# Second cross attention's keys and values from high and low parts, with the gates' weights in a place that is already used

## The reference, cut to what matters

```python
x = x + L0_xattn(layernorm(x), ctx, ctx, mask)
x = x + L0_attn(layernorm(x))       # convolutions, delta rule by chunks of 32, gates by W_fuse1, mixing
x = x + L0_ffn(layernorm(x))        # 8 experts, the two best of each row
x = x + L1_xattn(layernorm(x), ctx, ctx)
x = x + L1_attn(layernorm(x))
x = x + L1_ffn(layernorm(x))        # 16 experts of 128 and a shared one
# L1_xattn: 16 heads of 16
k = ctx @ Wk.T + bk                 # keys and values of all 64 contexts:
v = ctx @ Wv.T + bv                 # this is what the change forms in another way
out = softmax(q @ k.T / 4) @ v @ Wo.T + bo
```

## Time and profile before

| what | us |
|---|---|
| median of 3 runs (lowest, highest) | 1621.93 (1618.51, 1623.67) |
| span of the profiled execution | 1609.7 |
| TensorE busy | 1490.3 (93%) |
| VectorE busy | 1100.2 (68%) |
| ScalarE busy | 813.9 (51%) |
| GpSimd busy | 583.5 (36%) |
| keys' and values' matmuls (L386 and L390), busy | 121.5 + 117.2 |

### The profile page before, as it was taken

How to read it: one execution, slowest core, us unless ns; L and a number is a source line. 1 busy time by engine, 2 the same in 40 slices (tenths; PEclk the granted TensorE clock), 3 DMA queues, 4 the chain that set the end, 5 groups by cost and what they waited for, 6 DMA issues and landing times. The chain is left out here.

```text
span 1609.7 us, 38473 instructions
## 1 busy us (share of the span) xinstructions
PE 1490.3 (93%) x15176; PEld 1144.1 (71%) x15176; DVE 1100.2 (68%) x2412; ACT 813.9 (51%) x1848; POOL 583.5 (36%) x487
## 2 busy tenths in 40 slices
PE   5998999989988999999999989999899788999998
PEld 3454468544456579999998646666688686799997
DVE  4588869974047456666563558888599676767887
ACT  1233742121143336666654449999277422766663
POOL 2440310000011026777645346787288452121210
PEclk9899999999999999999999989999999999999999
DMA  9993048532024357676658317664000010010001
GB/s 327 316 354 97 1 156 219 133 73 46 1 80 137 110 209 278 217 274 239 237 181 222 96 50 246 204 209 129 27 1 1 18 30 15 1 34 21 27 1 53
DMA packets 114074, 203.99 MB, mean 127 GB/s; under 512 B 38073, under 2 KB 74361, under 8 KB 108009
## 3 DMA queue, kind: packets, MB, share of 16 engines
q1 hardware_dynamic: 91481, 107.72, 22.5%
q0 software_dynamic: 10032, 57.55, 10.3%
q10 hardware_dynamic: 12384, 36.27, 6.8%
HBM read 161.67 MB, written 39.83 MB: 125 GB/s over the span
## 5 line engine op out<-in xcount | busy, mean ns | idle before, releaser
L2387 POOL TENSOR_TENSOR a_pr<-a_pr,a_inv 128x1028 f32<-128x1028 f32 x64 | 122.2, 1909 | 63.6 <-DVE a_inv L2515 63.6
L386 PE MATMUL ps<-kv_ctx,kv_w 128*128 128x257 f32 x464 | 121.5, 397 | 8.5 <-ACT kv_kv L410 3.0
L390 PE MATMUL ps<-kv_w,kv_ctx 128*128 128x256 f32 x464 | 117.2, 397 | 8.3 <-ACT kv_kv L410 8.3
L2479 ACT ACTIVATE a_pr<-ps,a_neg 128x257 f32<-128x257 f32 x256 | 119.0, 473 | 2.7 <-DVE a_neg L2531 2.3
L2531 DVE TENSOR_REDUCE a_neg<-ps 128x2 f32<-128x514 f32 x128 | 87.9, 688 | 41.9 <-PE ps L2404 40.9
L1631 POOL TENSOR_TENSOR b0m_pm<-b_dr,b_gates 128x256 f32<-128x256 f32 x16 | 13.2, 829 | 279.3 <-SPq L1595 250.4
L390 PEld LDWEIGHTS ps<-kv_w,kv_ctx 128*128 128x128 f32 x464 | 89.4, 199 | 28.8 <-ACT kv_kv L410 14.6
L386 PEld LDWEIGHTS ps<-kv_ctx,kv_w 128*128 128x128 f32 x464 | 86.7, 197 | 26.8 <-issue 13.6
L3389 DVE SCALAR_TENSOR_TENSOR x<-ps,g_gate,x 128x256 f32<-128x256 f32 x256 | 105.1, 475 | 0.0
L972 DVE SCALAR_TENSOR_TENSOR b_F<-b_F,b_fir 128x992 f32<-128x992 f32 (+29 forms) x128 | 96.7, 792 | 0.0
L2415 PE MATMUL ps<-ident,a_pr 128*128 128x128 f32 x512 | 81.2, 281 | 16.3 <-ACT a_prT L2486 10.9
(11 more groups left out here) (447 smaller groups left out, 4433.1 us busy)
## 6 DMA issues: line engine op xcount, KB each, us to landing
late_kv<-kv SPq DMA_DIRECT2D x52, 513.0 KB, 4.4
kv<-kv_kv ACTq DMA_DIRECT2D x46, 513.0 KB, 5.4
a_ctxT<-in_ctxT SPq DMA_DIRECT2D x32, 514.0 KB, 9.7
a_ctxR<-in_ctx SPq DMA_DIRECT2D x32, 512.0 KB
kv_ctx<-in_ctxT ACTq DMA_DIRECT2D x34, 257.0 KB, 3.4
kv_ctx<-in_ctxT SPq DMA_DIRECT2D x24, 257.0 KB, 4.6
outs<-f_yo SPq DMA_DIRECT2D x16, 256.0 KB, 4.5
a_vB<-vlast SPq DMA_DIRECT2D x32, 128.0 KB
```

The source lines that it names most:

```text
L386: done = e.matmul(out[:, 0:NK], self.w[:, 0, c, cols(part)], ctx[:, c, :], start=(c == 0), stop=(c == DC - 1))
L390: done = e.matmul(out[:, cols(t, D)], ctx[:, c, cols(t)], self.w[:, 1, c, :], start=(c == 0), stop=(c == DC - 1))
L2387: e.tensor_tensor(pr[:, b % RP, :, :], pr[:, b % RP, :, :], inv[:, b % 2, :].unsqueeze(2).to_broadcast([P, HG, NK]), ALU.mult).then_inc(*p ...
L2479: e.activation(pr[:, b % RP, r, :], K.ps[:, bank(b, r), 0:NK], ACT.Exp, bias=neg[:, b % 2, r:r + 1], accum_out=tot[:, b % 2, r:r + 1]).the ...
```

## The change

The context and the two weights of the second cross attention's keys and values are split into high and low parts, and `product3` forms each product of a batch: 24 products of type float32r in place of 8 in float32, the keys' with 258 columns (`WIDTH`), the last of them zero.

- The raw weights are loaded ahead of the contexts of tile 14 in the first attention; GpSimd copies them to the high part and subtracts.
- For every context ScalarE rounds it into a high part (`round_to`), and GpSimd, or VectorE in the experts' tail (`low_by_dve`), subtracts for the low part (`low`). There are two places of parts (`LEAD = 2`), three in the router. ScalarE rounds a batch after the eviction of the batch two before it.
- TensorE waits for the low part in place of the load. The context's next load waits for it too, and ScalarE issues it behind the batch's store.
- The places of parts take 8 KB a partition. For them `W_fuse1` no longer has a tile of its own in `delta_solve`: it goes into `qk[:, 2:4]`, which the gram tiles read, and SP issues its load behind all stores of pairs and loads of A and M and behind the last gram tile. The squares and one row of the projections also go into tiles in use.
- In `delta_solve` GpSimd makes 20 low parts, in `delta_mix` one for each pair of tiles. In `experts_0` low parts stand between its gathers. In the experts' tail VectorE makes one low part behind each gather sum, and the two places of parts lie in the experts' weights.

SP's queue in `delta_solve`, before. (In what follows, `x4` counts like rows; a name behind "waits" is the semaphore waited for, named by who used it first, as `dma_a0_4_keys1` for the landing of the pairs' stores.)

The diff, cut to its core:

```diff
-    SLOTS, MORE = 3, 3
+    SLOTS, MORE, LEAD = 3, 3, 2
     BY_SYNC, TAIL, QUERIES = sum(AHEAD[:3]) + SLOTS, sum(AHEAD[:4]), sum(AHEAD[:5])
+    WIDTH = NK + 1
     def __init__(self, Y):
         self.K, self.Y = Y.K, Y
-        self.w, self.bk = Y.sb("w", [P, 2, DC, D]), Y.sb("bk", [P, DC])
+        self.w = [Y.sb(f"w{n}", [P, 2, DC, D], F32R) for n in "HL"]
+        self.bk = Y.sb("bk", [P, DC])
         self.ctx = places(Y.sb("ctx", [P, self.SLOTS, DC, NK]))
...
                         for b in range(B)]
-        self.loaded = self.BY_SYNC
+        self.loaded = 0
         self.mm, self.ev = Y.sig("pe", "kv"), Y.sig("act", "kv")
+        self.high, self.w_split = Y.sig("act", "kvhigh"), Y.sig("pool", "kvw")
+        self.p_low, self.v_low = Y.sig("pool", "kvlow"), Y.sig("dve", "kvlow")
         self.own = [KvPlace(Y, at, f"kv{n}") for n, at in enumerate(places(Y.sb("kv", [P, 2, KV])))]
-        self.formed = self.taken = self.last = 0
-        self.hosts = []
+        self.formed = self.taken = self.last = self.rounded = self.lowered = 0
+        self.hosts, self.parts = [], []
+        self.low_by_dve = range(self.TAIL, self.QUERIES)
     def host(self, count, banks, kv):
...
         return [h for h in self.hosts if h[0] <= j][-1]
+    def split_into(self, first, places):
+        self.parts.append((first, places))
+    def split_of(self, b):
+        first, at = [x for x in self.parts if x[0] <= b][-1]
+        return at[(b - first) % len(at)]
+    def split_before(self, b):
+        first, at = [x for x in self.parts if x[0] <= b][-1]
+        return b - len(at) if b - len(at) >= first else None
+    def low_done(self, b):
+        early, n = min(b, self.TAIL - 1) + 1, self.QUERIES - self.TAIL
+        if b in self.low_by_dve:
+            return self.v_low.at(b - self.TAIL + 1)
+        return self.p_low.at(early if b < self.TAIL else b + 1 - n)
     def before(self, b):
...
         s = self.slot_of[b]
+        if self.before(b):
+            e.wait_ge(*self.low_done(self.before(b)[-1]))
         e.dma_start(self.ctx[s], self.K.ins["ctxT"][b // BT, :, b % BT, :, :]).then_inc(*self.ld_c[s].up(16))
+        self.loaded = b + 1
     def sync(self, e, n):
         for b in range(self.loaded, min(self.loaded + n, B)):
-            if self.before(b):
-                e.wait_ge(*self.mm.at(3 * self.before(b)[-1] + 3))
             self.load(e, b)
-            self.loaded = b + 1
-    def begin(self, e):
+    def load_weights(self, e, raw):
         for n, name in enumerate(("Wk", "Wv")):
-            e.dma_start(self.w[:, n, :, :], features(self.K.ins[f"L1_xattn_{name}T"])).then_inc(*self.ld_w.up(16))
+            e.dma_start(raw[:, n, :, :], features(self.K.ins[f"L1_xattn_{name}T"])).then_inc(*self.ld_w.up(16))
         e.dma_start(self.bk[:, :], self.K.ins["L1_xattn_bk"]).then_inc(*self.ld_w.up(16))
-        for b in range(self.SLOTS):
-            self.load(e, b)
+    def split_weights(self, e, raw):
+        e.wait_ge(*self.ld_w.at(48))
+        e.tensor_copy(self.w[0][:, :, :, :], raw[:, :, :, :]).then_inc(*self.w_split.up())
+        e.wait_ge(*self.w_split.at(1))
+        e.tensor_tensor(self.w[1][:, :, :, :], raw[:, :, :, :], self.w[0][:, :, :, :].bitcast(F32), ALU.subtract).then_inc(*self.w_split.up())
+    def clear(self, e, first):
+        for at in [x for x in self.parts if x[0] == first][0][1]:
+            for part in at:
+                e.memset(part[:, :, NK:self.WIDTH].bitcast(F32), 0.0)
+    def round_to(self, e, last):
+        for b in range(self.rounded, last):
+            raw, (high, _) = self.ctx[self.slot_of[b]], self.split_of(b)
+            e.wait_ge(*self.ld_c[self.slot_of[b]].at(16 * (len(self.before(b)) + 1)))
+            if self.split_before(b) is not None:
+                e.wait_ge(*self.mm.at(3 * self.split_before(b) + 3))
+            e.activation(high[:, :, 0:NK], raw, ACT.Copy).then_inc(*self.high.up())
+            self.rounded = b + 1
+    def low(self, e, last):
+        for b in range(self.lowered, last):
+            raw, (high, low) = self.ctx[self.slot_of[b]], self.split_of(b)
+            e.wait_ge(*self.high.at(b + 1))
+            e.tensor_tensor(low[:, :, 0:NK], raw, high[:, :, 0:NK].bitcast(F32), ALU.subtract).then_inc(
+                *(self.v_low if b in self.low_by_dve else self.p_low).up())
+            self.lowered = b + 1
     def pe(self, e, n):
...
             first, banks, _ = self.host_of(j)
-            s, many = self.slot_of[b], len(banks)
-            ctx, out = self.ctx[s], self.K.ps[:, banks[(j - first) % many], :]
+            many = len(banks)
+            ctx, out = self.split_of(b), self.K.ps[:, banks[(j - first) % many], :]
             if j == 0:
-                e.wait_ge(*self.ld_w.at(48))
+                e.wait_ge(*self.w_split.at(2))
             if part == 0:
-                e.wait_ge(*self.ld_c[s].at(16 * (len(self.before(b)) + 1)))
+                e.wait_ge(*self.low_done(b))
             if j - first >= many:
...
                 for c in range(DC):
-                    done = e.matmul(out[:, 0:NK], self.w[:, 0, c, cols(part)], ctx[:, c, :], start=(c == 0), stop=(c == DC - 1))
+                    done = product3(e, out[:, 0:self.WIDTH], [w[:, 0, c, cols(part)] for w in self.w], [x[:, c, :] for x in ctx],
+                                    c == 0, c == DC - 1)
             else:
...
                     for c in range(DC):
-                        done = e.matmul(out[:, cols(t, D)], ctx[:, c, cols(t)], self.w[:, 1, c, :],
-                                        start=(c == 0), stop=(c == DC - 1))
+                        done = product3(e, out[:, cols(t, D)], [x[:, c, cols(t)] for x in ctx], [w[:, 1, c, :] for w in self.w],
+                                        c == 0, c == DC - 1)
             done.then_inc(*self.mm.up())
...
             if part == 2:
-                if b + self.SLOTS < self.BY_SYNC:
-                    self.load(e, b + self.SLOTS)
+                self.round_to(e, min([b + 1 + self.LEAD, self.last // 3] + [x for x, _ in self.parts if x > b]))
                 e.wait_ge(*self.ev.at(j + 1))
                 place.store(e, self.K.kv[b])
+                for x in range(self.loaded, min(self.rounded + self.SLOTS, b + self.LEAD + self.SLOTS, self.BY_SYNC)):
+                    self.load(e, x)
+def split_places(t):
+    return [(t[:, s, 0], t[:, s, 1]) for s in range(t.shape[1])]
 def places(t):
...
                 for t in range(1, NT):
+                    if t == NT - 2:
+                        A.load_weights(e, wkv)
                     keys(t)
...
                     values(t)
+                A.sync(e, 2)
                 K.front.load(e)
-                K.keys.begin(e)
+                A.sync(e, A.SLOTS - 2)
             @block.gpsimd
             def _(e):
+                A.clear(e, 0)
                 e.wait_ge(*ld_vo.at(80))
...
         step = sb("step", [P, L * L // 4])
-        f1 = sb("f1", [P, 8, 512])
+        f1 = qk[:, 2:4, :].rearrange("p c (k n) -> p (c k) n", n=512)
         ld_f, d_AS, d_Mt = Y.sigs_of("dma", "f1 AS Mt")
...
             def _(e):
-                e.dma_start(f1[:, :, :], features(K.ins["L0_attn_W_fuse1"])).then_inc(*ld_f.up(16))
                 for half in range(2):
...
                                         pairs[w, h, L * half:L * half + L, :, :]).then_inc(*ld_A[half].up(16))
+                e.wait_ge(*t_G.at(NT))
+                e.dma_start(f1, features(K.ins["L0_attn_W_fuse1"])).then_inc(*ld_f.up(16))
                 for half in range(2):
...
                 logits_back()
+            @block.gpsimd
+            def _(e):
+                ahead.low(e, ahead.formed // 3 + ahead.LEAD)
             @block.scalar
...
             def _(e):
+                ahead.low(e, ahead.lowered + 1)
                 for t in range(NT):
...
                     e.tensor_tensor(by_head(pm[:, t % 2, 3, :]), by_head(dr[:, t, :]), gate(t, 2), ALU.mult).then_inc(*p_p3.up())
+                    if t % 2:
+                        ahead.low(e, ahead.lowered + 1)
             @block.scalar
...
         stored = [(A.own + [kv2, kv3, kv1])[n % 5] for n in range(kept - first)]
+        low2 = w2[1][:, :, :, :].rearrange("p s f d -> p (s f d)")
+        size = 2 * DC * A.WIDTH
+        A.split_into(first - AHEAD[3], split_places(low2[:, 0:3 * size].rearrange(
+            "p (s w c k) -> p s w c k", s=3, w=2, c=DC)))
+        late = [w[:, BLOCKS % 2, :, :].rearrange("p f d -> p (f d)")[:, 0:size].rearrange("p (w c k) -> p w c k", w=2, c=DC) for w in w2]
+        A.split_into(first, [(x[:, 0], x[:, 1]) for x in late])
         A.host(AHEAD[4], (0, 1, 2, 3), stored + K.late.places(kept, first + AHEAD[4]))
...
                             token[:, FIRSTS[j] + n:FIRSTS[j] + n + 1], 0)).then_inc(*ld_x[j % 4].up(16))
+                A.clear(e, A.TAIL - AHEAD[3])
+                A.low(e, A.TAIL - 2)
                 e.wait_ge(*v_row.at(3))
...
                 gather1(1)
```

(3 more changed lines are left out.)

39 lines of the change are left out of this document (33 added, 6 removed).

## The result

| | before | after |
|---|---|---|
| median of 4 runs, us | 1621.93 | 1654.28 |
| lowest and highest | 1618.51, 1623.67 | 1653.98, 1666.61 |
| span of the profiled execution | 1609.7 | 1651.8 |
| TensorE busy | 1490.3 (93%) | 1465.9 (89%) |
| GpSimd busy | 583.5 (36%) | 663.8 (40%) |

The medians are 32 us apart, where 28 were forecast. The ratio is 1.0227, 95% interval 1.0188 to 1.0266, which is 30 to 43 us. The two profiled executions are 42 us apart: that of before has the shortest span that any of its executions showed, 12 us under its median time, while that of the change lies 2.5 us under its own.

The account below looks back on a forecast made before the run. TensorE was taken as the bound from 300 to 454, VectorE nearly full in the gram tiles, no engine full in the mixing. Terms summed to +28 us on the 1609.7 span; keeping 12.2 to the median gave 1650, range 1631 to 1667.

Parts of the forecast that it names:

- Solve stage to the outputs: Delta attention's solve: W_fuse1 issued at 297, landing at 306.5, outputs at 356 against 334.32; +22, plus 1 for restart.
- The 14 parts: Solve stage: key and value parts queued behind the W_fuse1 wait, paced by stores; 17 us, against 13.4 at bare rate.
- GpSimd against VectorE: Gram tiles: 11 GpSimd subtractions at 0.8 us a meeting, less 2.9 of idle, delay VectorE's chain by 6 us.
- The lock rule: Shared port pair locked per instruction when VectorE reads two SBUF inputs and GpSimd reads SBUF; some 2.5 us more if strict.
- First attention's end: Window 120 to 147: roundings behind the second norm's root, then subtractions, less 1.2 us of cheaper products; +1.5 (0 to 3).
- Mixing: Gates' mixing: TensorE's V part 0.3 us shorter over 8 pairs, one GpSimd subtraction fitting each pair; -2.5 (-4 to +4).
- Every meeting costs: Second rival: GpSimd and VectorE meetings cost a full microsecond, also in mixing and router, 16 more places; 1662 us, chance 0.16.
- Router: Token rows' gather waits behind batch 44's subtraction, 5.9 us later; 10 parts give about 2 back; together +6 (0 to +9).
- Tail: FFN's tail, 848 to 902: TensorE waits for VectorE's subtraction behind a gather sum, then cheaper batches; +1 (-6 to +5).
- Later four parts: Later in the solve stage: four more key and value parts run behind TensorE's work; -0.8 us.
- W_fuse1 comes early: Rival: faster loads of A and M, no lock, 14 parts nearer bare rate, gather moves little; +12, 1634 us, chance 0.25.
- Not what the change says: Rival: 258-column products might run at the present products' rate, 1.7 us more a batch; 1695 us, chance 0.02.

Follow-up runs that it names:

- late_fuse_alone: Kernel before, with only W_fuse1 moved into the place of queries and keys and issued last on SP: ratio 1.0121 against before.
- fuse_load_first: Changed kernel, SP issues W_fuse1 behind the second half's pair stores, ahead of its loads of A and M: ratio 1.0108 against before.
- load_first_wait_22: Changed kernel, W_fuse1 issued ahead of the second half's loads of A and M, TensorE's wait for it behind all 22 parts: ratio 1.0159 against before.
- no_low_read: Changed kernel, for batches 4 to 33 GpSimd writes zeros in place of the subtraction: median 1654.53 us, ratio 1.0103 against before.
- all_orders_mended: Changed kernel, W_fuse1 first and awaited after 22 parts, mixing subtraction later, token gather earlier, first attention's roundings before the last root: 1637.57 us, ratio 1.014 against before.
- mixing_low_later: Changed kernel, each GpSimd subtraction in the mixing put behind the next tile's product instead of ahead of it: ratio 1.0178 against before.
- router_and_tail: Changed kernel, token rows gathered ahead of batch 44's subtraction, three more low parts on VectorE ahead of the tail's first gather sum: ratio 1.0211 against before.
- plain_from_34: Changed kernel, batches 34 to 63 formed in float32 from the raw context without rounding or subtraction: median 1645.65 us, ratio 1.0161 against before.

## Why the prediction was right

The direction, the size (1650 forecast, 1654.28 measured) and the place and cause of the largest term were right; single terms were off on both sides, and the agreement within 4 us is in part luck. The terms were summed against the profiled span of before, and +28 on it makes 1637.7; the changed span was 1651.8. A to F are 43.9 us longer, where the forecast's terms for them add up to 27.7. The 12.2 us that I kept between the span and the median made up for most of that, since they came from a short profiled execution. Measured terms are differences of the stretches of after and before, where nothing else is said.

- *Solve stage to the outputs, forecast +23 with the restart* (outputs at 356). They began at 356.07, with some luck. The issue was forecast at 297 and came at 295.44, the landing at 306.5 and came at 306.04 as TensorE saw it. But of the 21.8 us of shift 3.4 had come from the stages ahead, which I had left out of this sum, and the gram tiles gave 3.7 where I had 6. C itself is +14.6, where 17 was left of the forecast. The cause is shown by late_fuse_alone (+16.7 with this part alone) and fuse_load_first (-7.8 for an issue 9 us earlier behind the last gram matmul).
- *The 14 parts at 17 us, the 8 at 12*: 18.8 (306.04 to 324.86) and 11.0 (345.05 to 356.07). Of the 18.8, the bare rate is 13.4. 3.2 us are products that started 0.21 us apart instead of 0.12 in the first 6 us (granted clock 0.56 there), where I had 1 us for a cold restart; 2.0 us are four gaps, three of them ended by an eviction. None of ScalarE's waits in it is put down to a store, so "paced by the stores" was not the reason here; it was in load_first_wait_22.
- *GpSimd against VectorE, 0.8 us a meeting*: the 48 taps behind the 16 gram tiles took 52.6 us against 44.5 before, 8.1 us more for 11 subtractions. It is not spread evenly: nine taps are 0.8 to 1.0 us longer each, a tenth 0.2, the others none. 3.7 us of it reached the end of the gram tiles in this trace, 5.2 by the means of nine traces and three, where I had 6. VectorE's own idle time in B shrank from 3.0 to 1.5 us, and the last of the 48 taps began 5.6 us later than before, counted from the first gram matmul: part of the 8.1 us lies behind the end of B.
- *The lock rule* (the Trainium skill, SBUF — State Buffer, "Who interferes with whom"): the trace agrees. The addition at 505.14 took 1.29 us beside the subtraction, 0.42 without, and beside the memsets of no_low_read, which read no SBUF, the taps were as short as before (0.945 us on the mean). One thing it would not lead one to expect: GpSimd's 128x256 product, started 0.05 us behind VectorE's second addition, which also has two SBUF inputs, left that at 0.43 us (508.51) and took 0.86 itself.
- *First attention's end, +1.5 (0 to 3)*: the next stage's first matmul is at 150.31 against 147.27, but the last output product had come 2.1 us earlier, so the stage's end is +5.1, outside my bounds (A, with the projections, is +5.5; their +0.5 fits). TensorE waited 4.10 us for the first subtraction, which stood behind the roundings behind the root, about as forecast. What failed is "less 1.2 us of cheaper products": the two batches took 9.9 us (138.24 to 148.13) instead of 7.8 (136.28 to 144.07), since behind the wait the products started 0.21 us apart until 144, at the lower of the two levels of the granted clock (1.2 GHz; the 0.50 third from the end of the row), and one wait of 1.22 us for an eviction stood between them:

```profile
138.00:144.00 6.00, 5.76 (x27) 5.79 (x28) 5.86 (x17) 1.19 (x3) 1.42 (x2) 0.50 0.00 0
```

  In all_orders_mended, with the roundings ahead of the root, there is no such wait, the starts are 0.12 us apart at once, and A is 85.5.
- *Mixing, -2.5 (-4 to +4)*: +4.6, the wrong sign. The step that failed is "GpSimd fits one subtraction into each pair": it fits in time, but not beside the two additions. My second rival had named this place. mixing_low_later and no_low_read both give it back (72.6 and 71.7), and no more than 1.5 us of the -2.5 shows then.
- *Router, +6*: F is +11.1. The place was right, the gather behind batch 44's subtraction: 8 us later behind the naming matmuls, where I had 5.9 (6.4 of them came back when it went ahead). Here my sum was short by its own prices: the eviction at 598.46, a rounding and a subtraction (0.60 + 0.6 + 1.04) end at 600.7, not at 599.5, 7.1 us later. What was sized wrong besides is that the 10 parts would give 2 back; the stretch ahead of the naming matmuls was 3 us longer instead (54.7 against 51.6).
- *Tail, +1 (-6 to +5)*: about +6 by the means. The wait forecast was there (5.41 us for VectorE's subtraction behind the first gather sum, after which matmuls started 0.22 us apart instead of 0.12 for a while), but taking it away gave nothing. In router_and_tail VectorE stood 7.6 us for a rounding instead. My reading is that the chain of landing, rounding, subtraction and gather sum on VectorE holds the tail; which link of it costs most was not told apart.
- *Queries and ramp, -0.5*: they lie in J, which reads 704.6 to 713.5 over all kernels, and can't be seen.
- *Later four parts, -0.8*: D is +4.4 in the change and -1.2 in fuse_load_first with the same code. In the change the granted clock is 0.86 in the 24 us behind the outputs' start and 0.90 in the last 24 before the mixing; in fuse_load_first both are 1.00. All traces go this way: D is 128.2 to 128.4 in the three where both rows read 1.00, 129.4 and 129.8 where one does (the two traces of before), and 131.6 to 133.8 in the eight where neither does. So D goes with the clock in these rows. Whether the change makes it lower is open: all eight are kernels with the split, and with the same code plain_from_34 and fuse_load_first read 1.00.

Of the rivals, "W_fuse1 comes early" fell with the issue at 295.44 and the longer taps, and "faster" with the landing at 306, where it wanted one near 284. "Every meeting costs" was right on the mixing, but its 12 us more than the forecast did not come in the medians. "Not what the change says" fell too: a batch's matmuls start 0.12 us apart at the full clock and TensorE is busy 24 us less in all. Those 24 us are on no path that sets the time.
